# Cross-attention and a routed feed-forward layer: scatters ahead of O_lo, choice and tables between two halves of P, four parts of 16 batches

## The reference, cut to what matters

```python
# x: (64, 128, 128)   ctx_768: (64, 77, 96)   16 heads of 64   8 experts, top 2, inner 176
x = x + attention(layernorm(x), ctx_768) @ w_out + b_out
x2 = layernorm(x).reshape(8192, 128)
logits = x2 @ router_w.T
_, idx = top_k(softmax(logits), 2)
gate = zeros.at[rows, idx].add(logits at idx)
moe = sum over 8 experts e of gate[:, e] * (silu(x2 @ w1[e].T) * (x2 @ w3[e].T)) @ w2[e].T
moe += (silu(x2 @ sw1.T) * (x2 @ sw3.T)) @ sw2.T          # the shared expert
return x + moe
```

## Time and profile before

| | |
|---|---|
| median of 3 runs | 1050.55 us (1046.46 to 1054.25) |
| the profiled execution | 1049.61 us, span 1047.7 us |
| PE, DVE, POOL, ACT busy | 948.9, 837.6, 748.1, 647.4 us |
| attention's iterations | to about 730 us |
| feed-forward on PE | about 735 to 1001 us |
| gathers on POOL | 833.08 to 1039.9 us |
| mean granted TensorE clock | 0.964 |

### The profile page before, as it was taken

One profiled execution on the slowest core, in us unless ns is written; L12 is line 12 of the kernel. 1 busy time (PEld: TensorE's weight loads), 2 busy tenths in 40 slices (PEclk: granted clock), 3 DMA queues, 4 the chain that ended last, 5 costly groups with the idle time before them and its releaser, 6 DMA issues.

```text
span 1047.7 us, 28760 instructions
## 1 busy us (share of the span) xinstructions
PE 948.9 (91%) x9838; PEld 799.4 (76%) x9838; DVE 837.6 (80%) x1904; ACT 647.4 (62%) x1354; POOL 748.1 (71%) x1121
## 2 busy tenths in 40 slices
PE   7899999999999999999999999988699999999910
PEld 6677778788878788778778787866499999987710
DVE  5898989989999998999899999899455556656721
ACT  4676779877777777767777777766234444453300
POOL 5345546767778778767877877887644588888887
PEclk9999999999999999999999999998799999999965
DMA  9154223253342323322434434254346576677421
GB/s 269 47 167 105 51 47 70 46 145 70 62 80 57 82 60 71 70 57 58 82 78 83 79 59 81 60 138 88 75 136 184 156 194 183 169 169 151 141 89 60
DMA packets 222733, 106.55 MB, mean 102 GB/s; under 512 B 160464, under 2 KB 214384, under 8 KB 221456
## 3 DMA queue, kind: packets, MB, share of 16 engines
q1 hardware_dynamic: 214400, 87.91, 35.9%
q0 software_dynamic: 8192, 16.79, 5.9%
HBM read 38.59 MB, written 34.60 MB: 70 GB/s over the span
## 4 chain that ended last, share of the span: by engine, by line
PE 38%; DVE 33%; POOL 13%; issue 9%; ACT 4%; DMA 3%; SPq 0%; DVEq 0%; POOLq 0%; ACTq 0%
POOL ctx_raw L582 9%; DVE top L983 7%; DVE pt_lo L1024 6%; DVE P L993 6%; PE Q L1273 5%; PE W L1137 3%; PE W L1138 3%; POOL ctx_raw L592 3%; PE W L1139 3%; PE S L1205 3%; DVE v_lo L1000 3%; PE W L1381 2%; PE S L1260 2%; PE W L1382 2%; DMA OT_lo<-O_lo 2%
## 5 line engine op out<-in xcount | busy, mean ns | idle before, releaser
L529 POOL TENSOR_TENSOR O_lo<-O,O_hi 128x512 f16<-128x512 f32 x128 | 145.6, 1157 | 162.8 <-ACT O_hi L696 162.8
L1024 DVE TENSOR_TENSOR pt_lo<-Q,pt_hi 77x512 f16<-77x512 f32 x256 | 164.0, 679 | 38.3 <-ACT pt_hi L688 37.5
L478 POOL DMA_INDIRECT xs<-x2cat,pos x128 | 133.0, 1039 | 61.7 <-DMA xs<-x2cat,pos 30.9
L688 ACT ACTIVATE pt_hi<-Q 77x512 f16<-77x512 f32 x256 | 144.4, 589 | 28.0 <-PE Q L1273 27.5
L664 ACT ACTIVATE v_hi<-W,sc 77x512 f16<-77x512 f32 x128 | 87.7, 686 | 117.2 <-PE W L1139 116.4
L1273 PE MATMUL Q<-ident,P 128*77 128x128 f32 x1024 | 148.3, 278 | 2.2 <-ACT P L671 0.8
L582 POOL DMA_INDIRECT ctx_raw<-ys,pos_y x128 | 132.1, 1032 | 23.3 <-issue 21.2
L1205 PE MATMUL S<-G,xTm 128*128 128x462 f32 (+1 forms) x384 | 143.2, 508 | 0.0
L1260 PE MATMUL S<-v_hi,pt_hi 96*128 96x65 f16 x1024 | 109.8, 197 | 28.9 <-DVE P L993 25.9
L1260 PEld LDWEIGHTS S<-v_hi,pt_hi 96*128 96x128 f16 x1024 | 93.9, 97 | 49.5 <-DVE P L993 44.5
L1273 PEld LDWEIGHTS Q<-ident,P 128*77 128x77 f32 x1024 | 122.1, 149 | 3.5 <-issue 2.4
(11 more groups left out here) (256 smaller groups left out, 2902.8 us busy)
## 6 DMA issues: line engine op xcount, KB each, us to landing
ys<-ysb SPq DMA_DIRECT2D x44, 256.0 KB
xg_early<-xs SPq DMA_DIRECT2D x60, 128.0 KB
xp<-x2cat SPq DMA_DIRECT2D x64, 64.0 KB, 1.9
y_out<-X SPq DMA_DIRECT2D x16, 256.0 KB
xg_late<-xs SPq DMA_DIRECT2D x28, 128.0 KB
xs<-zero_in SPq DMA_DIRECT2D x24, 128.0 KB, 2.5
X<-x_in SPq DMA_DIRECT2D x1, 2240.0 KB, 8.2
xs<-x2cat,pos POOLq DMA_INDIRECT x128, 3.0
```

The costliest lines, as they stand in the source:

```text
L478: pool.indirect_dma_start(out=xs_d[batch_part(b)][:, :], out_offset=index(pos, b, k), in_=x2cat[:, b % RING, :], in_offset=None).then_inc( ...
L529: pool.tensor_tensor(O_lo[:, half_], O[:, (t + 1) % 2, half_], O_hi[:, half_], ALU.subtract).then_inc(s["p_Olo"], 1)
L688: act.activation(pt_hi[0:NK, j % 2, c * 512:(c + 1) * 512], QB[q_bank(j, c)][0:NK, :], ACT.Copy).then_inc(s["a_PThi"], 1)
L1024: dve.tensor_tensor(pt_lo[0:NK, j % 2, c * 512:(c + 1) * 512], QB[q_bank(j, c)][0:NK, :], pt_hi[0:NK, j % 2, c * 512:(c + 1) * 512], ALU.s ...
```

## The change

- Four parts of 16 batches instead of 24, 24 and 16. `ROUTED` becomes 12, 12, 12 and 12: 48 routed groups instead of 44, and one more list in DRAM whose 1 MB edge block is zeroed early.
- DVE: the quarter of the choice, which stood between `moments` and `pt_low(2)`, and the piece of the tables, which stood at the end of the iteration, both stand between `pt_low(0)` and `pt_low(1)`. While attention runs, tables use only iterations with t mod 8 in 1 to 4, so a part's 12 pieces are spread wider.
- POOL: the two scatters stand ahead of `O_low` instead of behind it. The low part of the context (`cg_lo`) moves from DVE to POOL, behind `O_low`.
- After attention a batch's scatters wait only for the first scatter of the batch before, and for both of 8 batches before.
- The last chunk is chosen in two iterations instead of four and placed two iterations sooner.
- ACT and DVE do `slot(65)` behind their work on group 0 instead of ahead of it, PE does `project(65)` in feed-forward iteration 0 instead of 1, and the clearing of `hC` (1.34 us on DVE) goes to POOL, with `hC` and `hA` exchanged in SBUF.

```diff
-PART = [24, 24, 16]
+PART = [16, 16, 16, 16]
+SCR = 8
...
         HR = 3
+        hC = sb("hC", [128, HR, NT])
         hA = sb("hA", [128, HR, NT])
-        hC = sb("hC", [128, HR, NT])
...
-        names += [f"sc{r}" for r in range(RING)] + ...
+        names += [f"sc{k}_{r}" for k in range(2) for r in range(SCR)] + ...
...
-        TAB_SLOT = [CB * c + S_PLACE + 2 for c in P_END]
+        TAB_SLOT = [CB * c + S_PLACE + 2 - (2 if c == NCH - 1 else 0) for c in P_END]
         TAB_PIECES = 12
-        TAIL = max(NB + S_SCATTER, TAB_SLOT[-1] + TAB_PIECES)
+        TAB_AT = []
+        for first in TAB_SLOT:
+            first = max(first, TAB_AT[-1][-1] + 1 if TAB_AT else 0)
+            TAB_AT.append([t for t in range(first, NB + 6 * CB) if t % CB in (1, 2, 3, 4) or t > NB][:TAB_PIECES])
+        TAIL = max(NB + S_SCATTER, TAB_AT[-1][-1] + 1)
...
+        SOONER = 2
+        PLACE_AT = {CB * c + S_PLACE - (SOONER if c == NCH - 1 else 0): c for c in range(NCH)}
+        CHOOSE_AT = {}
+        for c in range(NCH):
+            for k in range(4):
+                CHOOSE_AT.setdefault(CB * c + S_CHOOSE + (k // 2 if c == NCH - 1 else k), []).append((c, k))
...
         def scattered(eng, b):
-            wait(eng, f"sc{b % RING}", 32 * (b // RING + 1))
+            for k in range(2):
+                wait(eng, f"sc{k}_{b % SCR}", 16 * (b // SCR + 1))
...
-                    i = t - TAB_SLOT[p] - TAB_PIECES + 2
+                    i = t - TAB_AT[p][8] - 2
...
             def scatters(t):
...
                     if t > LAST:
-                        scattered(pool, b - 1)
+                        wait(pool, f"sc0_{(b - 1) % SCR}", 16 * ((b - 1) // SCR + 1))
+                    if b >= SCR:
+                        scattered(pool, b - SCR)
                     scatter(b, 0); scatter(b, 1)
...
+            def context_low(t):
+                pool.wait_ge(s["a_cg"], (t + 8) // GB)
+                pool.tensor_tensor(cg_lo[:, :], ctx_raw[:, (t + 4) * NK:(t + 4 + GB) * NK], cg_hi[:, :].bitcast(F),
+                                   ALU.subtract).then_inc(s["p_cg"], 1)
...
+                scatters(t)
                 if on(t, 1, NB + 1):
                     O_low(t)
-                scatters(t)
+                if on(t + 1, 0, NB - GB) and t % GB == GB - 1:
+                    context_low(t + 1)
                 if on(t - 4, 0, NB):
                     x2_low(t)
...
             for t in range(FIRST, LAST + 1):
                 slot(t)
+                if t == NB:
+                    pool.wait_ge(s["s_S"], 3 * NB)
+                    pool.memset(hC[:, :, :].rearrange("p r n -> p (r n)"), 0.0).then_inc(s["hC_zero"], 1)
...
         @block.scalar                                    (the loop over groups; VectorE has the same two edits)
-            for t in range(FIRST, LAST + 1):
+            for t in range(FIRST, LAST):
                 slot(t)
...
-                if n > 0 and LAST + n <= TAIL:
+                if LAST + n <= TAIL:
                     slot(LAST + n)
...
         @block.vector
                 if on(t, 0, NB):
-                    pt_low(0); pt_low(1)
+                    pt_low(0)
+                for c, k in CHOOSE_AT.get(t, []):
+                    choose(c, k)
+                for p in range(NP):
+                    if t in TAB_AT[p]:
+                        tables(p, TAB_AT[p].index(t))
+                if on(t, 0, NB):
+                    pt_low(1)
                 if on(t, -2, NB + 3):
                     moments(t)
-                for piece_ in range(4):
-                    if chunk_of(t, S_CHOOSE + piece_) is not None:
-                        choose(chunk_of(t, S_CHOOSE + piece_), piece_)
...
-                if on(t + 1, FIRST, NB - GB) and j == GB - 1:
-                    context_low(t + 1)
                 if on(t, 0, NB):
                     pt_low(2); pt_low(3)
...
-                for p in range(NP):
-                    if on(t - TAB_SLOT[p], 0, TAB_PIECES):
-                        tables(p, t - TAB_SLOT[p])
...
             dve.wait_ge(s["s_O"], 3 * NB)
-            dve.memset(hC[:, :, :].rearrange("p r n -> p (r n)"), 0.0).then_inc(s["hC_zero"], 1)
...
         @block.tensor
                 def g_piece(k):
                     if k == 0:
-                        wait(pe, "d_cg", (t + 8) // GB)
+                        pe.wait_ge(s["d_cg"], 1)
+                        wait(pe, "p_cg", t // GB + 1)
...
-                if n == 1:
+                if n == 0:
                     project(LAST)
```

43 lines of the change are left out of this document (20 added, 23 removed).

## The result

The change made the kernel slower by a little: 1060.0 us (median of 7 runs, 1057.71 to 1060.47) against 1051.82 for the kernel before on the same chip, ratio 1.0078 [1.0053, 1.0102]. The forecast was 1044.5, a gain of 6 us, which is within 1% of no change but on the faster side; its range (1012 to 1070) held the time. Two later sets on other chips gave the changed kernel 1.0075 [1.0044, 1.0105] and 1.0065 [1.0039, 1.0090], so a loss of 7 to 8 us (0.7 to 0.8%) is firm. The profiled execution has a span of 1058.4 us, 10.6 over that of before. The chain of waits has the same shape as the earlier trace rows, with 2% less POOL in it.

A forecast was written before the change was run, and what follows sets the result against it. It took a PE-DVE loop to bound attention and the start of POOL's gathers to set the end. Terms -18 + 17 - 3.5 - 3 + 1.5 = -6.0 us on 1049.61 gave 1043.6, 1044.5 as a median; range 1012 to 1070.

The forecast's parts named there:

- the fourth list of zeros: At t = 4, one more MB of zeros on the queue carrying O's transposes, and more rows to turn: +1.5 us.
- the transition: From attention to the first gather: PE's wait for hC goes as slot(65) and project(65) move: -4.5 us.
- The loop: In attention, a loop through PE and DVE of 9.89 us against PE's 10.37, leaving 0.48 us between the low halves.
- Who wins the tie: At O_lo's start, the choice's second instruction, 0.04 us ahead, gets through in 0.22 us; the third stands behind the first half.
- choice gets past O_lo: Rival: in attention all three choice instructions run free, an iteration of 10.62 us, total 1015.5 us; chance 0.20.
- The choice's term, +17: Choice between the low halves makes its iterations 11.45 us instead of 10.84, +2.4 a chunk, seven chunks in attention: +17 us.
- a rival for all chunks: Tie lost: second and third choice instructions both stand behind O_lo, an iteration of 12.55 us, total 1075 us; chance 0.18.
- The scatters' place: In attention, scatters ahead of O_lo don't move O_lo; x2_low and the variance work come 2.5 us sooner, worth nothing.
- Tables, -3: In attention, tables' pieces between the low halves cost 6.5 us, against 8.0 plus perhaps 1.5 before: net -3 us.
- cg_lo, -3.5: In attention, moving cg_lo from DVE to POOL spares seven plain iterations 0.3 to 0.7 us each: -3.5 us.
- Scatter wait, -17.6, and +4: After attention, waiting for the first scatter only saves 1.26 us over 14 batches, -17.6; 4 us given back for the last chunk.
- for the old parts there was none to gain: Before the first gather: with the old parts, gathers started when the scatters were done, not when group 15 was.

The follow-up runs named there:

- e5: Changed kernel with GpSimd starting O_lo only when VectorE's quarter of the choice or its tables work is done: 1029.4 us, ratio 0.9795.
- e4: Changed kernel with the four lists' edge blocks zeroed one per iteration at t = 22 to 25: 1102.55 us, where the kernel before took 1070.12.
- e7: Changed kernel with the choice back behind the moments, O_lo held, and the zero lists written one each at t = 22 to 25: 1018.7 us, ratio 0.9685.
- h2: Changed kernel with the tables' pieces alone back at the end of VectorE's iteration: 1058.5 us, ratio 1.0068.
- g, three parts: Changed kernel with three parts of 24, 24 and 16 batches: 1063.0 us, ratio 1.0097.
- the two anchors: Changed kernel itself, run again in two later sets on other chips: 1058.6 us (ratio 1.0075) and 1058.5 us (1.0065).

## Why the prediction was wrong

The mechanism of the choice was right almost to the row, and the sign still came out wrong. The forecast was a small difference of large terms, and of its errors all the large ones went the same way. In the profiled runs attention is 11.9 us longer than forecast and the tail gives 3.1 us less.

**The step that failed** is the price of the fourth list of zeros: +1.5 us, with bounds 0 and 4, where iteration 5 grew by 7.0 us in this run and by 3.3 to 7.2 in the others. TensorE's wait for the transposed low half of O behind those lists, 5.04 us instead of 0.38, is what the forecast left out. Next to it stand the end of attention, t = 60 to 62, which grew by 5.2 us and had been priced like the iterations in the middle, and the transition, priced at -4.5 us and not found.

- **The loop.** Right in kind, its room too large: 0.34 us, not 0.48. The loop is 10.02 us rather than 9.89, since pt_low(2) starts 1.44 us behind the end of the second low half (276.67 to 278.11) where 0.07 + 1.26 = 1.33 were assumed. The pushed time is 1.60 rather than 1.56. So a choice iteration is 11.62 and not 11.45. The same 10.02 plus the pushed time gives the iterations with a piece of the tables (t = 34: 1.66 pushed, 11.68 measured).
- **Who wins the tie.** Right: L915 ahead by 0.03 us takes 0.23, L916 takes 1.07. Here the trace agrees with the Trainium skill (SBUF — State Buffer, section on the two separate sides), by which whichever of the two engines starts first gets the port pair for the whole instruction. The rival *choice gets past O_lo* is out; e5 brings it about by hand, at 1029 rather than 1015.5.
- **The choice's term, +17.** A chunk takes 46.30 us against 43.36, +2.9 instead of +2.4. Six whole chunks lie in attention (t = 13 to 56), not seven; the seventh has two quarters there, t = 61 and 62, which grew by 3.6 us together, in part because O_lo comes 0.4 us earlier behind v_lo and both instructions stand. The forecast had named that state as a rival for all chunks, and never asked in which iterations O_lo comes early. Undoing the edit gives -23.0: some 14 in the six chunks, 4.5 at t = 61 and 62, 4 in the tail, where the other two quarters lie (at t = 63 L915 takes 0.83 us and L916 1.08, at t = 64 both run free), and the rest elsewhere.
- **Fourth list, +1.5, bounds 0 and 4.** Iteration 5 takes 14.8 to 18.7 us against 11.55, and in e4 and e7, with all four lists written later, 11.0. The cost was taken as bytes on a queue. What the rows show is a transpose whose issue behind them takes 10.17 us of SyncE's time, and TensorE waits for the result. Bytes don't give the length either: with the same four lists it varies by 4 us from kernel to kernel, and why stays open.
- **The scatters' place, worth nothing.** Wrong twice. It costs some 0.6 us a chunk, as the earlier `x2_low` meets the choice even with the choice back. And against its undo it is worth 12 us, but most of that shields the tables piece and GpSimd's later work, which the kernel before didn't have to be shielded from. I priced the edits one at a time against the kernel before, and this one pays only beside another.
- **Tables, -3.** The six iterations with a blocked piece (t = 34, 35, 50, 58, 59, 60) are 7.3 us over the like without one, against 6.5 forecast for all and 9.5 before: -2 rather than -3. h2 shows that the place between the halves is not what saves.
- **cg_lo, -3.5.** Not tried alone. In the trace t = 3, 27 and 51 fall by 0.44 to 0.49 us, t = 11 and 19 by 0.09 (at 35, 43 and 59 the tables mix in), so -2 to -3.
- **Transition, -4.5.** Not found: undoing it moves the tail by nothing. One wait of TensorE went and another of 1.74 us came.
- **Scatter wait, -17.6, and +4.** The last scatter came 10.6 us nearer with three parts (110.8 to 100.2) and 13 to 15 with four, where 17.6 + 4.5 - 4 = 18 were forecast. The spacing came out right (3.7 against 3.6 us). The tail's term as a whole was -18 and measured -14.9, in its bounds. The forecast's remark that *for the old parts there was none to gain* was right, and g, three parts, shows how: 11.63 us of wait for the store.
- **The sum.** Forecast +12 in attention and -18 behind it; measured +23.9 and -14.9, and a start 2.2 us later that is no part of the change. In the two anchors attention is at +20 and +21. That the time fell inside the range of 1012 to 1070 says little: the range was wide enough for three different mechanisms.

## What to carry to other kernels

Before moving work of one engine, look at what the engine that can block it does at the new instant, in every kind of iteration, the first and last ones above all. Here the cheap remedy was not a move: a wait that holds the partner's uncritical instruction for half a microsecond was worth 29 us with the choice between the halves, and some 10 more on top of the 23 of moving the choice back (ratio 0.9739 against 0.9838, in two sets). The hold on the kernel before was not run. And a queue that carries a latency-critical transfer every iteration should get bulk issues one at a time: spreading the lists of zeros took 7.4 us out of iteration 5, spreading the early loads 2 us out of iteration 62. An edit can change another's worth: four parts brought 4.5 us in the changed kernel and 9.6 once the lists were spread and the choice was out of O_lo's way.

## What the runs showed of the hardware

A two-operand VectorE instruction on 8 elements a row stood for 2.97 us behind four GpSimd instructions in a row (0.15 us when free), so a blocked one does not always get through between two: L960 passed neither the gap ahead of xb nor the one between the halves of O_lo, while in the earlier trace rows one did. What decides that stays open. A TENSOR_SCALAR with one tile operand and a column of scalars (L939) is blocked as well (910 against 247 ns), and so is one with a single tile operand of 24 elements in one row (L977 and L978 at t = 60: 1.02 and 1.08 us, 0.16 and 0.17 in e5); the reductions beside them were not (L914, 0.20 us). A DMA transpose was issued in 1.23 us on a free queue, in 4.00 behind 3 lists of zeros and in 10.17 behind 4. And one chip ran the gathers with 0.42 us of idle ahead of each instead of 0.19, 30 us over the kernel, with the instruction itself unchanged.
